# The opening of a routed mixture: logits in column tiles, weight splits between routing steps, one product on VectorE

## What is computed

```
def _L0_ffn_ref(x, gate_w, gate_bank, up_bank, down_bank):
    K = 2
    logits = jnp.einsum('btd,ed->bte', x, gate_w)
    probs = jax.nn.softmax(logits, axis=-1)
    selected_probs, selected_idx = jax.lax.top_k(probs, K)
    selected_probs = selected_probs / (jnp.sum(selected_probs, axis=-1, keepdims=True) + 1e-08)
    a = jnp.einsum('btd,edh->bteh', x, gate_bank)
    u = jnp.einsum('btd,edh->bteh', x, up_bank)
    h = jax.nn.silu(a) * u
    y_all = jnp.einsum('bteh,ehd->bted', h, down_bank)
    y_sel = jnp.take_along_axis(y_all, selected_idx[..., None], axis=2)
    y = jnp.sum(y_sel * selected_probs[..., None], axis=2)
    return y
...
t = _to_tokens(x)
t = t + _L0_ffn_ref(_ln_t(t), L0_ffn_gate_w, L0_ffn_gate_bank, L0_ffn_up_bank, L0_ffn_down_bank)
```

## Time and profile before

| | us |
|---|---|
| median of 3 runs | 3370.66 (3368.36 to 3373.05) |
| the profiled execution | 3370.78 |
| its span in the profile | 3368.9 |
| TensorE busy | 2764.8 (82%) |
| VectorE busy | 2414.6 (72%) |
| ScalarE busy | 1860.7 (55%) |
| GpSimd busy | 435.2 (13%) |

### The profile page before, as it was taken

One profiled execution on the slowest core, in us unless ns is written; L12 is line 12 of the kernel. 1 busy time (PEld: TensorE's weight loads), 2 busy tenths in 40 slices (PEclk: granted clock), 3 DMA queues, 4 the chain that ended last, 5 costly groups with the idle time before them and its releaser, 6 DMA issues. The chain is left out here.

```text
span 3368.9 us, 62705 instructions
## 1 busy us (share of the span) xinstructions
PE 2764.8 (82%) x18708; PEld 1277.7 (38%) x18708; DVE 2414.6 (72%) x4597; ACT 1860.7 (55%) x2592; POOL 435.2 (13%) x513
## 2 busy tenths in 40 slices
PE   5948999997499239589999956199999959599999
PEld 3612222226499126222222234022222236366666
DVE  6458999974766354579999955589999835465665
ACT  4416777773255124167777736067777736465554
POOL 0010111111333510101111110201111100000000
PEclk9759999996699667599999977599999979699999
DMA  2555776664122214567766701101111110200000
GB/s 64 169 125 114 151 148 142 148 126 143 33 78 76 70 31 146 134 110 150 149 146 149 145 22 50 57 28 52 48 48 49 48 32 1 55 22 5 9 5 14
DMA packets 202070, 277.27 MB, mean 82 GB/s; under 512 B 54302, under 2 KB 93454, under 8 KB 201930
## 3 DMA queue, kind: packets, MB, share of 16 engines
q1 hardware_dynamic: 162346, 211.32, 27.1%
q0 software_dynamic: 19920, 31.57, 4.0%
q10 hardware_dynamic: 19664, 32.60, 3.3%
HBM read 196.93 MB, written 77.46 MB: 81 GB/s over the span
## 5 line engine op out<-in xcount | busy, mean ns | idle before, releaser
L750 DVE TENSOR_REDUCE c1att_mx<-c1att_m 128x1 f32<-128x512 f32 x768 | 493.4, 685 | 35.7 <-PE c1att_m L688 30.6
L750 DVE TENSOR_REDUCE c0att_mx<-c0att_m 128x1 f32<-128x512 f32 x768 | 493.4, 685 | 32.5 <-PE c0att_m L688 27.2
L750 DVE TENSOR_REDUCE f1att_mx<-f1att_m 128x1 f32<-128x512 f32 x768 | 493.3, 685 | 26.5 <-PE f1att_m L688 21.8
L996 ACT ACTIVATE c1att_p<-c1att_s 128x1024 f32<-128x1024 f32 x384 | 373.9, 1020 | 152.0 <-PE c1att_s L703 151.9
L996 ACT ACTIVATE c0att_p<-c0att_s 128x1024 f32<-128x1024 f32 x384 | 373.9, 1020 | 148.8 <-PE c0att_s L703 148.7
L996 ACT ACTIVATE f1att_p<-f1att_s 128x1024 f32<-128x1024 f32 x384 | 373.9, 1020 | 143.8 <-PE f1att_s L703 142.8
L1426 ACT ACTIVATE moe_h<-moe_u,moe_bu 128x512 f32<-128x512 f32 x192 | 136.5, 711 | 175.6 <-PE moe_u L1343 93.9
L688 PE MATMUL f1att_m<-f1att_km,f1att_qm 16*128 16x512 f16 x768 | 155.7, 401 | 88.6 <-DVE f1att_ka L959 52.9
L716 PE MATMUL f1att_o<-f1att_p,f1att_vs 128*32 128x512 f32 x1536 | 206.2, 609 | 0.6 <-ACT f1att_p L996 0.6
L716 PE MATMUL c0att_o<-c0att_p,c0att_vs 128*32 128x512 f32 x1536 | 206.2, 609 | 0.6 <-ACT c0att_p L996 0.6
L716 PE MATMUL c1att_o<-c1att_p,c1att_vs 128*32 128x512 f32 x1536 | 206.1, 609 | 0.6 <-ACT c1att_p L996 0.6
(11 more groups left out here) (608 smaller groups left out, 5430.8 us busy)
## 6 DMA issues: line engine op xcount, KB each, us to landing
xt<-rel_parts SPq DMA_DIRECT2D x256, 128.0 KB, 5.0
xt<-qk_parts SPq DMA_DIRECT2D x192, 128.0 KB, 4.4
y<-rel_parts SPq DMA_DIRECT2D x128, 128.0 KB, 5.6
y<-qk_parts SPq DMA_DIRECT2D x96, 128.0 KB, 5.1
c0att_qm<-rel_parts SPq DMA_DIRECT2D x144, 64.0 KB, 2.1
c1att_qm<-rel_parts SPq DMA_DIRECT2D x144, 64.0 KB, 2.1
expert_rows<-y SPq DMA_DIRECT2D x39, 192.0 KB, 2.0
o_sums<-c0att_o ACTq DMA_DIRECT2D x24, 256.0 KB, 4.3
```

The costliest lines, as they stand in the source:

```text
L750: dve.tensor_reduce(mx[:, n:n + 1], bank[:, :], AX.X, ALU.max).then_inc(s_mx, 1)
L996: act.activation(pr[h][kt % 2][:, :], sps[h][:, :], ACT.Exp).then_inc(s_e, 1)
```

## The change

- Logits: `gw` is padded to 32 columns with zeros (two memsets on GpSimd, for which SP's first load waits), and is now the weight side; 512 tokens of one chunk stream past it. Four chunks go to four groups of 32 columns of TensorE and so to four groups of 32 partitions of one bank. `logits(0)` stands behind the transposes of chunk 4, `logits(1)` behind all. The result lies experts by tokens; ScalarE copies it to SBUF (`logits_out`), TensorE transposes it (`logits_back`), and VectorE gathers it into `key` with 4 copies a call. The routing reads `key`. A one-element memset ends the chain of those copies.
- Splits: ScalarE makes the high parts of blocks 0 to 2 behind chunks 2, 4 and 6, and 3 to 7 behind the exponential. VectorE splits 0 to 2 ahead of the routing, 3 and 4 between `top` and the wait for the ranks, 5 and 6 behind `owner`, 7 behind `give`.
- Raw tiles: a fifth one in the last part of `rows`. SP loads four blocks ahead of the writes of `xn`, then block 4 (in tile 0), block 5 (in the fifth tile, once `xn` is written and all chunks are transposed), 6 and 7.
- `by_pick` moves from GpSimd to VectorE; `lo_hot` goes ahead of `by_place`.
- TensorE's wait for all splits moves behind the first transposes of the loop.

```diff
     AHEAD = 3
     mats = (gate_bank, w_up)
     SPLITS = 2 * len(mats) + 1
-    RAWS = 4
+    PLACE, USES = (0, 1, 2, 3, 0, 4, 2, 3), (0, 0, 0, 0, 1, 0, 1, 1)
+    RAWS = 5
     RAW = 4 * bw + mt * C
     UNITS = 4
     xn, yd = scratch["xn"], scratch["yd"]
...
         raw_d = [t[:, 4 * bw:RAW] for t in spare]
-        gw = [m.sb("gw0", experts), m.sb("gw1", experts, parts=C1)]
+        gw = [m.sb("gw0", 32), m.sb("gw1", 32, parts=C1)]
...
 
+                sp.wait_ge(s_pad, 2)
                 for t, src in zip(gw, (w_gate[0:C0, :], w_gate[C0:C, :])):
-                    sp.dma_start(t[:, :], src).then_inc(s_gw, 16)
-                for blk in range(RAWS - 1):
+                    sp.dma_start(t[:, 0:experts], src).then_inc(s_gw, 16)
+                for blk in range(4):
                     load_weights(blk)
                 sp.dma_start(upper[:, :], a["upper"]).then_inc(s_const, 16)
                 sp.dma_start(place[:, :], a["place"]).then_inc(s_const, 16)
@@ -1659,9 +1678,12 @@
                     sp.wait_ge(s_norm, 4 * n + 4)
                     sp.dma_start(xn[n * CHUNK:(n + 1) * CHUNK, :].rearrange("(t p) f -> p t f", p=P),
                                  rows[:, n * 4 * C:(n + 1) * 4 * C].rearrange("p (t f) -> p t f", t=4)).then_inc(s_xn, 16)
-                for blk in range(RAWS - 1, experts):
+                load_weights(4)
+                sp.wait_ge(s_xn, 16 * (T // CHUNK))
+                sp.wait_ge(s_turn, T // CHUNK)
+                load_weights(5)
+                for blk in (6, 7):
                     load_weights(blk)
-                sp.wait_ge(s_xn, 16 * (T // CHUNK))
                 for b in range(BLOCKS):
                     u = b % AHEAD
                     sp.wait_ge(s_y, b + 1)
...
             def _(pool):
+                for i, t in enumerate(gw):
+                    pool.memset(t[:, :], 0.0).then_inc(s_pad, 1)
+                    pool.wait_ge(s_pad, i + 1)
                 for i, t in enumerate(bl):
                     pool.memset(t[C1:P, :], 0.0).then_inc(s_pad, 1)
-                    pool.wait_ge(s_pad, i + 1)
+                    pool.wait_ge(s_pad, i + 3)
                 pool.memset(ones[:, :], 1.0).then_inc(s_pad, 1)
-
-                pool.wait_ge(s_const, 48)
-                pool.wait_ge(s_xn, 16 * (T // CHUNK))
-                pool.wait_ge(s_hot, 2)
-                pool.tensor_tensor(by_pick.rearrange("p (k s) -> p k s", s=SLOTS),
-                                   hi_hot.rearrange("p (k s) -> p k s", s=SLOTS),
-                                   table[:, COUNT:COUNT + PAIR].unsqueeze(2).broadcast_to([P, PAIR, SLOTS]),
-                                   ALU.mult).then_inc(s_picks, 1)
+                pool.wait_ge(s_pad, 5)
 
                 def fetch(b):
                     u = b % AHEAD
...
 
-                def logit(n):
-                    pe.wait_ge(s_f32, 2 * n + 2)
-                    for j in range(4):
-                        t = 4 * n + j
-                        for k, c in enumerate((C0, C1)):
-                            ins = pe.matmul(logits[:, t * experts:(t + 1) * experts], room[k][0:c, t * P:(t + 1) * P],
-                                            gw[k][0:c, :], start=k == 0, stop=k == 1)
+                def logits(i):
+                    pe.wait_ge(s_f32, 8 * i + 8)
+                    for k, c in enumerate((C0, C1)):
+                        for j in range(4):
+                            ins = pe.matmul(banks[4 + i][32 * j:32 * j + 32, :], gw[k][0:c, :],
+                                            room[k][0:c, (4 * i + j) * CHUNK:(4 * i + j + 1) * CHUNK],
+                                            start=k == 0, stop=k == 1)
                     ins.then_inc(s_lg, 1)
+
+                def logits_back(i):
+                    pe.wait_ge(s_lgc, i + 1)
+                    for t in range(4):
+                        ins = pe.transpose(banks[6 + i][:, t * P:(t + 1) * P], raw_lg[i][:, t * P:(t + 1) * P], ident)
+                    ins.then_inc(s_lgt, 1)
 
                 pe.wait_ge(s_gw, 32)
                 for n in range(T // CHUNK):
-                        logit(n - 1)
-                logit(T // CHUNK - 1)
+                    if n == 4:
+                        logits(0)
+                    if n == 6:
+                        logits_back(0)
+                logits(1)
+                logits_back(1)
...
                     ins.then_inc(s_down, 1)
 
                 pe.wait_ge(s_owner, 1)
+                transposes(0)
                 pe.wait_ge(s_wl, SPLITS * experts)
-                transposes(0)
                 before = None
                 for b in range(BLOCKS):
...
                                    scale=W_SCALE).then_inc(s_wh, 1)
+
+                def logits_out(i):
+                    act.wait_ge(s_lg, i + 1)
+                    act.activation(raw_lg[i], banks[4 + i][:, :], ACT.Copy).then_inc(s_lgc, 1)
 
                 act.wait_ge(s_chain, 6)
                 act.activation(std[:, :], var[:, :], ACT.Sqrt).then_inc(s_std, 1)
@@ -1832,13 +1863,14 @@
                     cols = slice(n * CHUNK, (n + 1) * CHUNK)
                     for k, (tile, c) in enumerate(((t0[n % 2], C0), (t1[n % 2], C1))):
                         act.activation(room[k][0:c, cols], tile[0:c, :], ACT.Identity).then_inc(s_f32, 1)
-                    if n % 2:
-                        split_high(n // 2)
-                for blk in range(T // CHUNK // 2, experts - 2):
-                    split_high(blk)
+                    if n == 4:
+                        logits_out(0)
+                    if n in (2, 4, 6):
+                        split_high(n // 2 - 1)
+                logits_out(1)
                 act.wait_ge(s_route, 1)
                 act.activation(key[:, :], cand[:, :], ACT.Exp).then_inc(s_exp, 1)
-                for blk in range(experts - 2, experts):
+                for blk in range(3, experts):
                     split_high(blk)
 
...
 
-                lg = cube(logits[:, 0:TILES * experts])
                 key3, cand3, first3, second3, slots3 = (cube(t[:, :]) for t in (key, cand, first, second, slots))
                 experts_row = table[:, COUNT:COUNT + experts].unsqueeze(1).broadcast_to([P, TILES, experts])
                 dve.wait_ge(s_const, 48)
-                dve.wait_ge(s_lg, T // CHUNK)
-                link(dve.tensor_reduce(one[:, :], lg, AX.X, ALU.max))
-                dve.tensor_tensor(cand3, lg, per_token(one[:, :]), ALU.subtract).then_inc(s_route, 1)
+                for i in range(2):
+                    dve.wait_ge(s_lgt, i + 1)
+                    to = key[:, i * 16 * experts:(i + 1) * 16 * experts].rearrange("p (j t e) -> p t j e", j=4, e=experts)
+                    source = banks[6 + i][:, :].rearrange("p (t j e) -> p t j e", t=4, j=4)
+                    for t in range(4):
+                        inc(dve.tensor_copy(to[:, t], source[:, t, :, 0:experts]))
+                link(dve.memset(low_one[:, 0:1], 0.0))
+                link(dve.tensor_reduce(one[:, :], key3, AX.X, ALU.max))
+                dve.tensor_tensor(cand3, key3, per_token(one[:, :]), ALU.subtract).then_inc(s_route, 1)
                 dve.wait_ge(s_exp, 1)
                 link(dve.tensor_reduce(one[:, :], key3, AX.X, ALU.add))
                 link(dve.reciprocal(one[:, :], one[:, :]))
@@ -1952,6 +1989,8 @@
                                        top[:, :].rearrange("p (k t) -> p k t", k=2),
                                        one[:, :].unsqueeze(1).broadcast_to([P, 2, TILES]), ALU.mult))
 
+                for blk in (3, 4):
+                    split_low(blk)
                 dve.wait_ge(s_rank, 1)
                 link(dve.tensor_tensor(full[:, :].rearrange("p (e j) -> p e j", j=16),
                                        counts[:, 0:experts].unsqueeze(2).broadcast_to([P, experts, 16]),
...
                 link(dve.scalar_tensor_tensor(out=slot_lo[:, :], in0=slot_hi[:, :], scalar=-float(P), in1=slot[:, :],
                                               op0=ALU.mult, op1=ALU.add))
-                dve.wait_ge(s_wl, SPLITS * (experts - 2))
                 dve.tensor_tensor(hi_hot.rearrange("p (k s) -> p k s", s=SLOTS),
                                   table[:, COUNT:COUNT + SLOTS].unsqueeze(1).broadcast_to([P, PAIR, SLOTS]),
                                   slot_hi[:, :].unsqueeze(2).broadcast_to([P, PAIR, SLOTS]), ALU.is_equal).then_inc(s_hot, 1)
-                dve.wait_ge(s_hot, 1)
-                dve.tensor_scalar(by_place, hi_hot, place[:, :], None, ALU.mult).then_inc(s_hot, 1)
+                dve.wait_ge(s_wl, 5 * SPLITS)
                 dve.tensor_tensor(lo_hot.rearrange("p (k s) -> p k s", s=P),
                                   table[:, COUNT:COUNT + P].unsqueeze(1).broadcast_to([P, PAIR, P]),
                                   slot_lo[:, :].unsqueeze(2).broadcast_to([P, PAIR, P]), ALU.is_equal).then_inc(s_hot, 1)
+
+                dve.wait_ge(s_hot, 2)
```

(7 more changed lines are left out.)

36 lines of the change are left out of this document (23 added, 13 removed).

## The result

| | before | changed |
|---|---|---|
| median, us | 3371.62 (4 runs) | **3351.14** (3349.38 to 3354.11, 4 runs) |
| ratio | 1 | **0.9939**, 95% interval 0.9923 to 0.9955 |
| profiled execution, us | 3370.78 | 3354.11 |
| its span | 3368.9 | 3352.2 |
| the mixture's stage, first `f_mean` to the next layer norm's mean | 409.56 | 388.80 |

The kernel is 20.5 us faster by the medians, against a forecast of 20.0 (3350.7 us). The two profiled executions lie only 16.7 us apart, since the changed one was the slowest of its four and came to this stage 3.7 us later. A later series of five runs on another chip gave 0.9933 (0.992 to 0.9947).

A forecast was written before the change was run, and what follows sets the result against it. The 108 us ahead of the expert loop were taken as a chain that bounds what the change can gain; 18.4 - 1.3 + 2.9 = 20.0 us, so 3370.7 - 20.0 = 3350.7 us, range 3344 to 3357.

The forecast's parts named there:

- Part 1: Opening of the mixture: logits in four column tiles, two calls, bring the first routing reduction from 852.4 to 834.0, gain 18.4 us.
- C: Rival on the logits calls: column tiles run one after another, 13.7 us a call, 3369.9 us, no change; chance 7%.
- D: Rival on the logits calls: serial and not pipelined, 24 us a call, kernel 20 us slower at 3390; chance 4%.
- so I stay near half: Opening: TensorE's clock taken near half, first reduction at 834.0; full clock throughout would give 829.8 or so.
- rival B: TensorE at 2.4 GHz in the opening, list 4.2 us sooner, 3346.5; sign: first reduction before 831; chance 10%.
- The PSUM copies: VectorE's four 32-element copies per logits call, taken at 0.2 us each; with the memset 0.9 us at the chain's end.
- Part 2: Splits moved: splits 3 and 4 between routing and rank wait cost 1.3 us, and the 3.78 us wait is gone.
- Split 7 beside the fetch: nothing: At the loop's start: split 7 behind `give`, 2.6 us beside the first fetch, costs nothing.
- Part 3: `by_pick` on VectorE: `hi_hot` to the list takes 27.1 us instead of 30.0, gain 2.9 us.
- Rival A: First fetches of the loop held by split 7, up to 2.6 us, 3353.3; chance 10%.
- Changes of shape: TensorE's switches of tile shape in the logits calls cost nothing; by the skill page some 0.6 us a call.
- The queues: SP's later writes of `xn`, raw tile loads and `gw` load cost nothing; cover for block 4 is 8 us.

The follow-up runs named there:

- split7_in_loop: Changed kernel with split 7 on VectorE moved from between `give` and the loop to behind the loop's first `x_low`; 3355.03 us, ratio 0.9951.
- split3_early: Changed kernel with split 3 in the wait for the second call of logits, 4 and 5 before the rank wait, 6 alone behind `owner`; 3351.32 us, ratio 0.9945.
- serial_call: Changed kernel with eight more matmuls behind the first call of logits, all into one column group of a bank that nothing reads; 3362.44 us, single run.
- after_again: The changed kernel run again unaltered in the second series, its second profiled execution; 3348.78 us, ratio 0.9933 to the kernel before.

## Why the prediction was right, and where it was lucky

- **Part 1** was undersized: 22.0 us (20.5 in the second execution, 20.5 to 22.0 in six) instead of 18.4. The mechanism is as stated, and only this: four tiles beside each other (C and D out), two calls, ScalarE ordering the opening. The step that was off is "so I stay near half". In both executions TensorE kept a granted clock of 1.00 through the 2.0 us of idle time ahead of the first call and the 3.0 us ahead of the second. In the profiled one it fell 1.5 us into the first call and 1.3 us into the second; in the other the first call ran at 1.00 to its end and the second at 0.50 from its start. The first call took 2.4 us to the next transpose instead of 4.1, the last 2.7. Over all executions with tiled calls the first took 2.06 to 2.93 us, the last 2.71 to 3.80. In the times of the kernel before, the last call began at 825.3 instead of 827.6 and ended at 828.0 instead of 831.7. The reduction at 830.4 fell under the 831 that I had named as rival B's mark; in the second execution it would be 831.9. B came half true. The reason against it, that ScalarE starves TensorE, did not decide: the idle time came and the clock was still 1.00 at the start of three of the four calls. Whether the idle time brings the later fall is open; before the change it fell by 816 with TensorE busy in the whole stretch ahead of it.
- Also missing from part 1 was what it rests on. The gain needs splits 3 to 5 moved (7.9 us without, 22.0 with), and moving them needs the faster logits. I costed the splits in part 2 at +1.3 and gave their departure from ahead of the reduction no line of its own. The sum came out since both were there.
- The PSUM copies: 4 in 0.48 us, one row; with the memset 0.54 from the first copy to the reduction, against my 0.9.
- **Part 2**: 14.21 against 14.14. The wait of 3.78 us is gone as stated. "Split 7 beside the fetch: nothing" was wrong: +0.85. "TensorE's wait for all splits: nothing" held, as split 7 ends 3.4 us ahead of the loop's first transpose (883.49 and 886.87); ended 5.3 us behind it, in `split7_in_loop`, it cost 3.9.
- **Part 3**: 26.91 against 27.1. `by_pick` 5.35, `past` 0.48; the second list matmuls began 0.06 us behind its end (873.36), and took 2.53 us at full clock instead of 4.23. Put back on GpSimd it costs 3.3 to 3.9 us ahead of the list. One term was missing: with `by_pick` gone from GpSimd the first fetch begins 0.6 us later behind `give`, and that the sum did not have.
- **Rival A** came true in part: over 7 us from list to loop, a first indirect DMA of 1.92 us, as its marks said. List to loop grew by 1.4 us; of that 0.85 is the longer DMA, which is this rival's price instead of 2.6, and 0.6 the late start, which stays without split 7. The reason is only half shown. With split 7 moved away from it the DMA takes 1.07 (four runs, and the one with the old order of splits), so split 7 is needed for the length. But in both runs with `by_pick` on GpSimd split 7 ran beside it, and it took 1.11 and 1.12. The Trainium skill, page "SBUF — State Buffer", section "Who interferes with whom", makes the port pair that VectorE and GpSimd share an exclusive lock. The 9.68 us of the TENSOR_SCALAR agrees. The same section infers that a `tensor_tensor`, which uses only the read side of the pair, does not hold up the making of a DMA's descriptors; split 7's operations have two SBUF inputs too (`scalar_tensor_tensor`), and for them the 1.11 agrees and the 1.92 does not. Split 7's own operations kept their 0.54 us throughout. What the second condition is stays open: those two runs differ in what GpSimd did before, and in how far the DMA starts behind split 7 (0.37 us, not 0.97), and no run separates the two. Small operations of GpSimd ahead of it are not enough.
- **Changes of shape**: the sum put them at nothing, by the transposes. In the calls each costs about 0.09 us at full clock (last section), too little to move the sum.
- **The queues**: no reader on the path waited. ScalarE did wait for raw tiles, a sign that I had named as one of error, but harmlessly:

```profile
842.29 0.52 ACT L1851 ACTIVATE f_ah<-y 128x384 f16<-128x384 f32 x1 [2.41 <-DMA y<-in_f_down]
```

  Its VectorE reader comes at 874.4. Split 5 can stand behind `owner` with so late a tile.
- **Behind the opening** the loop to the end took 1.5 us more (0.6 in the second execution). In the first the clock rose 2.6 us later than before the change; one execution of each does not make that a cost of the change, and `split3_early` shows 301.8 with the same start.

So 3351.14 against 3350.7 is partly luck, errors that cancel: 3.6 us too little gain in the opening, against 1.4 too little cost at the fetch (0.85 and 0.6) and 1.5 in the loop. The range and the chances held; the distances are the better test.

## What to carry to other kernels

When two things end close together ahead of a step (here TensorE's logits, and VectorE's splits with their raw tiles), price each with the other in its old and in its new place: here moving the splits alone brought nothing at the reduction, tiling the logits alone 7.9 us (with the new raw tiles), both together 22. A stall that is removed or filled is only worth the distance to the next arrival. Ask of a moved piece of work not when its engine is free, but who waits for its last result and what stands behind that wait. And compare stages by their distances from a common mark: here they showed a list 2.5 us sooner (24.36 and 26.91) where the medians of whole runs could not tell 3 us.

## What the runs showed of the hardware

- A granted clock of 1.00 survived 2.0 and 3.0 us of TensorE's idle time and fell 1.3 to 1.5 us into the call behind it, or with the start of that call. In one execution the first call took 2.06 us and the second, of the same shape, 3.80 ten microseconds on.
- A float32 record of 512 columns steps at 0.43 us in one column group at full clock, and 16 of them over four groups take 2.06.
- A change of shape costs about 0.09 us at full clock. In `serial_call` the first record of 64*32 begins 0.52 us behind the last of 128*32 (826.02 and 826.55), and the 128*128 transpose 0.52 us behind the last record (829.58 and 830.10), where records of one shape are 0.43 apart; at 826.54 the weight loads pause for 0.84 us instead of 0.32. In the tiled call of `after_again`, too, four records follow four others after 0.45 us within a shape and 0.54 across the change. So the transpose behind it starts 1.99 us after the call, of which about 0.2 are the two changes. The Trainium skill, page "TensorEngine Tiling (Array Packing)", section Key Properties, has each change of mode drain TensorE; the trace agrees, at a smaller price than the 0.6 us a call that the prediction worked out by it at half clock. The 1.00 us of the earlier trace rows also has such a change at its end.

```profile
826.02 0.59 PE L1742 MATMUL f_bank<-xt,f_gw 128*32 128x512 f32 x1
826.55 0.61 PE L1742 MATMUL f_bank<-xt,f_gw 64*32 64x512 f32 x1
827.00 0.59 PE L1742 MATMUL f_bank<-xt,f_gw 64*32 64x512 f32 x1
829.58 0.59 PE L1742 MATMUL f_bank<-xt,f_gw 64*32 64x512 f32 x1
830.10 0.33 PE L1758 MATMUL f_bank<-ident,y 128*128 128x128 f32 x1
```

- GpSimd's product of 4992 elements held VectorE's next operation to its end whichever it was (`past` of 312 elements in the kernel before, a TENSOR_SCALAR of 4992 here), while VectorE's 8.7 us `lo_hot`, which had begun 0.25 us ahead of the product, kept its length.
- GpSimd's first indirect DMA took 1.92 us instead of 1.07 beside VectorE's differences of two SBUF inputs, later ones 1.22 and 1.10 instead of 0.95, and 1.11 in a kernel in which GpSimd had made the product before. It began 0.5 us behind the start of `give` where GpSimd had made the product, and 1.1 us behind it where it had not.
